# Windowed attention on one core: GpSimd's low part of the exponential waits for VectorE's logits of the same step

## The chip, the cores and the metric

One core of a Trainium2 chip runs the whole program. The metric is the time of one execution in microseconds (us). The engines are TensorE (PE in the profile, its weight loads PEld), VectorE (DVE), ScalarE (ACT), GpSimd (POOL) and SyncE (SP), which here issues DMAs.

## What is computed

The program is a fake-quantised windowed attention on a 16x192x56x56 image, followed by a ConvNeXt block (7x7 convolution, layer norm, two products). The change is in the attention. Cut to that part, the reference is:

```
B, C, H, W = x.shape                      # 16, 192, 56, 56; windows of 7 x 7, 12 heads of 16
q = fq(q * SCALE); k = fq(k); v = fq(v)   # fq: round to 8 bits with one scale for the tensor
attn = jnp.einsum('bhmc,bhnc->bhmn', q, k)
attn = fq(attn) + bias[None]
attn = fq(attn)
attn = jax.nn.softmax(attn, axis=3)
out = jnp.einsum('bhmn,bhnc->bhmc', attn, v)
```

## The kernel before, in words

The program runs seven phases one after another: ranges of the input and of q, k and v, a second pass that writes them quantised, the attention, the output projection, the convolution and the two products of the block. There is no scheduler. Each engine has its own list of instructions, written by hand, and engines meet only at semaphores.

`phase_attention` (L759) works in 512 steps. A tile is two windows at once, on 98 of 128 partitions, with 12 heads x 49 = 588 columns. Each tile goes through a pipeline, and each engine does in step n what is written in its own `step(n, l, stage)`, for tiles of different age:

- PE, in this order: q·k of tile n into `p_psum` (L455), the logits with their maximum taken off of tile n-3 into `l_psum` (L875 to L879), the product with the values of tile n-6 into `o_psum` (L894, 24 matmuls), and the transposes of the logits of tile n-1 into `t_psum` (L903), from which the maximum is taken.
- ACT: the exponential of tile n-4 twice, once in float32 into `exp` (L922, two buffers) and once in float16 into `exp_hi` (L923, four buffers, semaphore `hid`), and then `attn_int` of tile n (L929, semaphore `a1d`), which rounds `p_psum` to 8 bits.
- DVE: `logit_int` of tile n-1 (L948, semaphore `a2d`), which adds the bias to `attn_int`; so the logits of tile n are made at the head of DVE's step n+1. Then the reciprocal of the sums (L957), a statistic of the output (L962), the normalised output `a_o` (L975, semaphore `nrm`) and the negative maximum `neg_max` (L981).
- POOL: `exp_lo = exp - exp_hi` of tile n-4, two instructions (L852, semaphore `lod`), as soon as `exp_hi` of that tile is there. POOL issues nothing else in this phase, no DMA either.

L948 reads two operands from on-chip memory (`attn_int` and `bias_products`), and L852 reads two as well (`exp` and `exp_hi`).

Who waits for `lod`: PE, before it multiplies tile n-6 by the values, and ACT, before it writes `exp` again, since there are only two such buffers. In ACT's step the latter is

```
m, r, bank = n - LAG_E, (l - LAG_E) % 4, (l - LAG_E) % 2
act.wait_ge(lgd, m + 1)
if stage(LAG_E + 2):
    act.wait_ge(lod, m - 1)
```

that is, the `exp` of tile n-4 needs `exp_lo` of tile n-6 (LAG_E is 4). SP loads q, k and v of 16 tiles at a time (a unit) and stores the output of a unit.

Of the kernel before, what the change touches and what calls it, by code (L numbers as in the profile page):

```python
# [60 lines left out]
def chain(eng, sem, start=0):  # L61

    count = [start]

    def link(ins):
        count[0] += 1
        ins.then_inc(sem, 1)
        eng.wait_ge(sem, count[0])
    link.count = count
    return link  # L70
# [47 lines left out]
def col(s, k, rows=P):  # L118
    return s.sc[0:rows, k:k + 1]
# [639 lines left out]
def phase_attention(s):  # L759
# [4 lines left out]
    with ExitStack() as c:  # L764
# [22 lines left out]
        zero, qk, a1d, a2d = s.sem("a_preset"), s.sem("a_qk_done"), s.sem("a1_done"), s.sem("a2_done")  # L787
# [7 lines left out]
        def steps(eng, step):  # L795

            def turn(i, first):
                for k in range(2):
                    for j in range(UP):
                        step(32 * i + 16 * k + j, 16 * k + j, lambda lag: not first or 16 * k + j >= lag)  # L800
            turn(0, True)
            with eng.Fori(0, (IMG - 1) // TURN) as t:
                for m in range(TURN):
                    turn(TURN * t + m + 1, False)
            for j in range(LAG_S):
                step(TAIL + j, j, lambda lag: lag > j)

        @blk.sync
        def _(sp):
            def store(u, k):  # L810
                sp.wait_ge(ostd, u + 1)
                for h in range(2):
                    sp.dma_start(s.od[bass.ds(u, 1)].rearrange("u h n j w f -> (u h) n j w f")[h], o[k][64 * h:64 * h + N]).then_inc(st[k], 16)

            def unit(i, first):
                for k in range(2):
                    u = bass.ds(2 * i + k, 1)
                    if not first:
                        sp.wait_ge(qk, UP * (2 * i + k - 1))
                    load_qk(s, sp, u, q[k], kt[k], ld[k])  # L820
                    if not first:
                        sp.wait_ge(pvd, UP * (2 * i + k - 1))
                    else:
                        sp.wait_ge(vzero, k + 1)
                    for w in range(2):
                        sp.dma_start(vt[k][64 * w:64 * w + N, w], s.vd[bass.ds(2 * i + k, 1)].rearrange("u o n j f -> (u o) n j f")[w]).then_inc(lv[k], 16)
                    if not first:
                        store(2 * i + k - 2, k)
            peeled(sp, IMG, unit)
            for k in range(2):  # L830
                store(UNITS - 2 + k, k)
            for k in range(2):
                sp.wait_ge(st[k], 32 * IMG)

        @blk.gpsimd
        def _(pool):
            link = chain(pool, zero)
            for m in eh:
                link(nc.gpsimd.memset(m[:], 1.0))
                link(nc.gpsimd.memset(m[:, :, 1], 0.0))  # L840
            for m in el:
                link(nc.gpsimd.memset(m[:], 0.0))

            def step(n, l, stage):
                if stage(LAG_E):
                    r, m = (l - LAG_E) % 4, n - LAG_E
                    pool.wait_ge(hid, m + 1)
                    if stage(LAG_E + 4):
                        pool.wait_ge(pvd, m - 3)
                    src = e[r % 2][:].rearrange("p (a b n) -> p b a n", a=2, b=6)  # L850
                    for a in range(2):
                        last = nc.gpsimd.tensor_tensor(el[r][:, :, 2 * a, 0:N], src[:, :, a], eh[r][:, :, 2 * a, 0:N], ALU.subtract)  # L852
                    last.then_inc(lod, 1)
            steps(pool, step)
            pool.wait_ge(ch, 3)
            nc.gpsimd.partition_all_reduce(col(s, T1), col(s, T0), P, RMAX).then_inc(ar, 1)
# [1024 lines left out]
```

## Time and profile before

| | |
|---|---|
| median of 3 runs | 5082.19 us (5073.92 to 5095.0) |
| the profiled execution | 5095.38 us, of which the span from first to last instruction is 5093.7 us |
| the attention's steps | from 1319.3 us to about 2467 us of the span |
| busy over the whole span | PE 79%, DVE 77%, ACT 64%, POOL 30% |
| granted TensorE clock, mean | 0.902 |

The times are of whole executions; the profile is of one of them. An instruction's row gives its start in the span, its duration, its engine and line, and the tiles that it writes and reads. Consecutive instructions of one kind with no idle time between them are merged into one row with their count. "Idle before" in brackets is the time in which the engine stood still just ahead of the row, and behind the arrow stands what ended it. On ACT and DVE an instruction starts a little before the one ahead of it has ended, so that starts lie closer together than durations add up to.

### The profile page before, as it was taken

To read this page: it belongs to the slowest core of one execution; us is meant where nothing else is said; L and a number is where in the kernel's file an instruction comes from. 1 tells how busy PE (TensorE), PEld (TensorE's weight loads), DVE (VectorE), ACT (ScalarE), POOL (GpSimd) and SP (SyncE) were. 2 spreads that over 40 slices of the span, in tenths; PEclk is the share of its full clock that TensorE was granted. 3 is DMA by queue.
4 is the path that set the end of the run, shared out by engine and by line. 5 is a ranking of instruction groups with operands and counts; after the bars stand their busy time and mean duration, and the time that the engine had idled before them with its cause. 6 is when DMAs were issued, how large, how long until landed. Compare 5 with 4: busy or idle time off the path is not lost. (4 is left out here: it accounts for less than half of the span.)

```text
span 5093.7 us, 116728 instructions
## 1 busy us (share of the span) xinstructions
PE 4027.8 (79%) x40394; PEld 2551.1 (50%) x40394; DVE 3922.3 (77%) x7112; ACT 3246.1 (64%) x5602; POOL 1504.5 (30%) x1844
## 2 busy tenths in 40 slices
PE   1687777676688988888456669996689999999999
PEld 1233554454577776777444434443345455554544
DVE  7797999999999999999645520001799999999985
ACT  0675777775698988989355644443556666666663
POOL 0201111111666666666422200001232222222210
PEclk9997777876799999999777779998799999999999
DMA  7773666665333333333277778886122222222212
GB/s 316 203 204 107 160 160 166 159 163 143 79 96 94 91 94 91 94 91 94 74 256 254 279 243 290 278 278 200 63 66 90 87 90 76 76 90 87 90 55 68
DMA packets 227952, 725.18 MB, mean 142 GB/s; under 512 B 30346, under 2 KB 128138, under 8 KB 206794
## 3 DMA queue, kind: packets, MB, share of 16 engines
q1 hardware_dynamic: 203402, 589.58, 39.6%
q0 software_dynamic: 24128, 130.26, 7.1%
q8 instruction: 230, 3.77, 0.3%
q14 instruction: 192, 1.57, 0.1%
HBM read 428.25 MB, written 291.50 MB: 141 GB/s over the span
## 5 line engine op out<-in xcount | busy, mean ns | idle before, releaser
L852 POOL TENSOR_TENSOR exp_lo<-exp,exp_hi 128x294 f16<-128x294 f32 x1024 | 773.1, 782 | 374.8 <-ACT exp_hi L923 374.8
L1613 PE MATMUL out_psum<-gelu_hi,w_parts 128*128 128x448 f16 x2016 | 605.0, 355 | 58.9 <-DVE w_parts L1789 31.5
L1649 ACT ACTIVATE gelu_pair<-h_psum,b_rows,w_unscale 128x448 f32<-128x448 f32 x448 | 324.5, 728 | 412.5 <-PE h_psum L1565 224.7
L1685 DVE BATCH_NORM_STATS2 ln_stats<-z_img 128x6 f32<-128x192 f32 x448 | 126.0, 344 | 566.7 <-DMA z_img<-zd 565.9
L1349 PE MATMUL conv_psum<-c_in,toeplitz 128*128 128x448 f16 (+1 forms) x2304 | 470.4, 366 | 68.9 <-DMA dwb<-in_L_conv_dw_b_dram 68.9
L948 DVE SCALAR_TENSOR_TENSOR logit_int<-attn_int,scalars,bias_products 128x588 f16<-128x588 int8 x512 | 488.2, 954 | 38.6 <-ACT attn_int L929 27.0
L1565 PE MATMUL h_psum<-ln_parts_T,w_hi 128*128 128x448 f16 x2016 | 494.3, 354 | 18.1 <-DVE w_in L1748 16.2
L929 ACT ACTIVATE attn_int<-p_psum,scalars 128x588 int8<-128x588 f32 x512 | 389.4, 761 | 174.7 <-PE p_psum L455 163.7
L1613 PE MATMUL out_psum<-gelu_lo,w_parts 128*128 128x448 f16 x1344 | 475.5, 354 | 0.0
L610 PE MATMUL range_psum<-q_diag,k_diag 128*128 128x196 bf16 x1536 | 275.2, 316 | 227.8 <-DVE p_min L692 225.0
L894 PE MATMUL o_psum<-a_v,exp_hi 128*128 128x34 f16 x6144 | 382.8, 179 | 78.4 <-DVE a_o L975 66.3
L1363 ACT ACTIVATE c_out<-conv_psum,dwb,conv_unscale 128x448 f32<-128x448 f32 x192 | 223.5, 1164 | 315.3 <-PE conv_psum L1349 315.3
L1506 POOL TENSOR_TENSOR ln_parts<-ln_out,ln_parts 128x512 f16<-128x512 f32 x224 | 257.4, 1170 | 504.0 <-DVE ln_parts L1713 504.0
L894 PEld LDWEIGHTS o_psum<-a_v,exp_hi 128*128 128x128 f16 x6144 | 338.0, 96 | 132.9 <-issue 93.3
L922 ACT ACTIVATE exp<-l_psum,scalars 128x588 f32<-128x588 f32 x512 | 388.0, 758 | 24.3 <-PE l_psum L879 13.5
L923 ACT ACTIVATE exp_hi<-l_psum,scalars 128x588 f16<-128x588 f32 x512 | 399.2, 780 | 0.0
L894 PE MATMUL o_psum<-a_v,exp_lo 128*128 128x34 f16 x6144 | 380.4, 178 | 20.4 <-issue 20.0
L1349 PEld LDWEIGHTS conv_psum<-c_in,toeplitz 128*128 128x128 f16 x2304 | 223.8, 98 | 315.3 <-issue 40.0
L650 ACT ACTIVATE qk_i<-qk_psum,qk_quant_scale 128x392 int8<-128x392 f32 x384 | 218.8, 586 | 249.1 <-PE qk_psum L589 241.3
L692 DVE TENSOR_TENSOR p_max<-range_psum,p_max 128x784 f32<-128x784 f32 x384 | 368.2, 959 | 7.2 <-PE range_psum L610 7.2
L692 DVE TENSOR_TENSOR p_min<-range_psum,p_min 128x784 f32<-128x784 f32 x384 | 368.2, 959 | 0.0
L610 PEld LDWEIGHTS range_psum<-q_diag,k_diag 128*128 128x128 bf16 x1536 | 186.7, 155 | 358.2 <-DVE p_min L692 346.4
(313 smaller groups left out, 9901.8 us busy)
## 6 DMA issues: line engine op xcount, KB each, us to landing
k_diag<-kd SPq DMA_DIRECT2D x128, 384.0 KB, 5.0
toeplitz<-gd SPq DMA_DIRECT2D x48, 1024.0 KB, 17.2
yd<-y_out POOLq DMA_DIRECT2D x16, 2880.0 KB, 28.1
c_in<-yd SPq DMA_DIRECT2D x24, 1920.0 KB, 9.4
zd<-c_out POOLq DMA_DIRECT2D x24, 1792.0 KB, 13.8
z_img<-zd SPq DMA_DIRECT2D x16, 2688.0 KB, 9.4
x_chunk<-in_x_dram SPq DMA_DIRECT2D x12, 3136.0 KB, 10.4
x_img<-in_x_dram SPq DMA_DIRECT2D x16, 2352.0 KB, 15.9
```

Of the source, the lines that this page charges most:

```text
L610: last = nc.tensor.matmul(ps[:, x % 2, y // 2, y % 2 * 256:y % 2 * 256 + HG * N], kt[k][:, g].rearrange("p o n -> p (o n)")[:, j::UP], q[k ...
L692: v.tensor_tensor(e[:, g], ps[:, x % 2].rearrange("p a (b c) -> p (a b) c", b=2)[:, :, 0:HG * N], e[:, g], op).then_inc(done, 1)
L852: last = nc.gpsimd.tensor_tensor(el[r][:, :, 2 * a, 0:N], src[:, :, a], eh[r][:, :, 2 * a, 0:N], ALU.subtract)
L894: last = nc.tensor.matmul(po[:, b * PV0:(b + 1) * PV0], x[r][:, b, a:a + 2].rearrange("p a n -> p (a n)"), rhs, start=a == 0 and x is eh, ...
L922: nc.scalar.activation(e[r % 2][:], pl[:, bank, 0:HM], ACT.Exp, scale=col(s, S2))
L923: nc.scalar.activation(eh[r][:, :, 0:3:2].rearrange("p b a n -> p a b n")[:, :, :, 0:N], pl[:, bank, 0:HM].rearrange("p (a b n) -> p a b n ...
L929: nc.scalar.activation(a1[l % 2][:].rearrange("p (g n) -> p g n", g=G), pp[:, 0:G, 0:HG * N], ACT.Copy, scale=col(s, CP)).then_inc(a1d, 1)
L948: v.scalar_tensor_tensor(a2[r][:], a1[(l - LAG_A2) % 2][:], col(s, RAT), s.bpart[:], ALU.mult, ALU.add).then_inc(a2d, 1)
L1349: last = nc.tensor.matmul(out[:, :, lo:hi], tp[k][:, w, ch, 2 - d, :], yi[k][:, :, ch, yy, lo + d:hi + d], start=x == 0 and part == 0, sto ...
L1565: last = nc.tensor.matmul(ph[:, y % 3, 0:TCH], w, xx, start=x == 0, stop=x == 4)
L1613: last = nc.tensor.matmul(po[:, t, 0:TCH], w, hx[:, f, cols], start=f == 0 and x == 0, stop=f == NF - 1 and x == len(steps) - 1)
L1649: nc.scalar.activation(h[y // 2 % 3][:, y % 2], ph[:, y % 3, 0:TCH], ACT.Gelu, scale=k1[:], bias=b1[:, f:f + 1]).then_inc(hd, 1)
```

## The change

In POOL's step, after the wait for `exp_hi` (`hid`) and the wait for a free `exp_lo` buffer (`pvd`), a wait for the logits of tile n (`a2d`, which L948 raises) is added. `stage(0)` holds in all 512 steps but the last eight that drain the pipeline. No instruction of any engine is added, removed or moved otherwise; the two instructions that were L852 become L854.

```
@@ -847,6 +847,8 @@
                     pool.wait_ge(hid, m + 1)
                     if stage(LAG_E + 4):
                         pool.wait_ge(pvd, m - 3)
+                    if stage(0):
+                        pool.wait_ge(a2d, n + 1)
                     src = e[r % 2][:].rearrange("p (a b n) -> p b a n", a=2, b=6)
                     for a in range(2):
                         last = nc.gpsimd.tensor_tensor(el[r][:, :, 2 * a, 0:N], src[:, :, a], eh[r][:, :, 2 * a, 0:N], ALU.subtract)
```

Here m is n-4, so POOL's work on tile n-4 now stands behind VectorE's work on tile n.

## Rows read from the trace of the kernel before

**Rows 1.** Windows view of the attention's steps: busy us (xinstructions) by engine, PEclk, DMA share, GB/s

```profile
1319.30:2467.00 1147.70, 1014.15 (x22498) 827.74 (x22499) 1075.85 (x2618) 1023.79 (x1535) 773.11 (x1024) 0.97 0.35 91
```

**Rows 2.** Groups by line, the attention's steps: xcount | busy us, mean ns | idle before, releasers

```profile
L852 POOL TENSOR_TENSOR exp_lo<-exp,exp_hi 128x294 f16<-128x294 f32 x1024 | 773.1, 782 | 374.8 <-ACT exp_hi L923 374.8
L948 DVE SCALAR_TENSOR_TENSOR logit_int<-attn_int,scalars,bias_products 128x588 f16<-128x588 int8 x512 | 488.2, 954 | 38.6 <-ACT attn_int L929 27.0 <-issue 9.2
...
L957 DVE RECIPROCAL sum_recip<-o_psum 128x12 f32<-128x12 f32 x511 | 113.3, 222 | 30.6 <-PE o_psum L894 29.8
```

**Rows 3.** The line of the logits: duration ns min/median/max, first and last start us

```profile
L948 DVE SCALAR_TENSOR_TENSOR logit_int<-attn_int,scalars,bias_products x512: 814/841/1401, 1319.3 to 2456.6; 128x588 f16<-128x588 int8 x171
```

**Rows 4.** Timeline of DVE, a free step and a held one

```profile
1972.90 0.82 DVE L948 SCALAR_TENSOR_TENSOR logit_int<-attn_int,scalars,bias_products 128x588 f16<-128x588 int8 x1
...
1973.99 0.33 DVE L975 TENSOR_TENSOR a_o<-o_psum,sum_recip 128x192 f32<-128x192 f32 x1
1974.25 0.65 DVE L981 TENSOR_REDUCE neg_max<-t_psum 128x10 f16<-128x490 f16 x1
1974.82 1.06 DVE L948 SCALAR_TENSOR_TENSOR logit_int<-attn_int,scalars,bias_products 128x588 f16<-128x588 int8 x1
...
1976.99 1.06 DVE L948 SCALAR_TENSOR_TENSOR logit_int<-attn_int,scalars,bias_products 128x588 f16<-128x588 int8 x1
```

**Rows 5.** Timeline of POOL at the same place

```profile
1973.84 1.42 POOL L852 TENSOR_TENSOR exp_lo<-exp,exp_hi 128x294 f16<-128x294 f32 x2 [0.77 <-ACT exp_hi L923]
```

**Rows 6.** Timeline of ACT at the same place

```profile
1973.00 0.77 ACT L923 ACTIVATE exp_hi<-l_psum,scalars 128x588 f16<-128x588 f32 x1
1973.89 0.75 ACT L929 ACTIVATE attn_int<-p_psum,scalars 128x588 int8<-128x588 f32 x1
1974.54 0.74 ACT L922 ACTIVATE exp<-l_psum,scalars 128x588 f32<-128x588 f32 x1
1975.18 0.77 ACT L923 ACTIVATE exp_hi<-l_psum,scalars 128x588 f16<-128x588 f32 x1
1975.82 0.75 ACT L929 ACTIVATE attn_int<-p_psum,scalars 128x588 int8<-128x588 f32 x1
```

**Rows 7.** Windows view, an early stretch of 10 us (columns as in rows 1)

```profile
1343.00:1353.00 10.00, 10.00 (x235) 8.22 (x231) 10.00 (x27) 10.00 (x17) 10.00 (x12) 1.00 0.47 100
```

**Rows 8.** Timeline of POOL around that stretch

```profile
1341.73 11.62 POOL L852 TENSOR_TENSOR exp_lo<-exp,exp_hi 128x294 f16<-128x294 f32 x12
```

**Rows 9.** Timeline around one of ACT's waits for POOL

```profile
1366.38 1.42 POOL L852 TENSOR_TENSOR exp_lo<-exp,exp_hi 128x294 f16<-128x294 f32 x2 [0.78 <-ACT exp_hi L923]
1366.43 0.75 ACT L929 ACTIVATE attn_int<-p_psum,scalars 128x588 int8<-128x588 f32 x1
...
1367.82 0.75 ACT L922 ACTIVATE exp<-l_psum,scalars 128x588 f32<-128x588 f32 x1 [0.64 <-POOL exp_lo L852]
```

**Rows 10.** Timeline, POOL released by DVE in a later phase

```profile
4009.78 0.56 DVE L1713 CAST ln_parts<-ln_out 128x768 f16<-128x768 f32 x1
...
4010.42 1.16 POOL L1506 TENSOR_TENSOR ln_parts<-ln_out,ln_parts 128x512 f16<-128x512 f32 x1 [6.71 <-DVE ln_parts L1713]
```

**Rows 11.** Timeline, DVE released by ACT

```profile
1796.27 0.75 ACT L929 ACTIVATE attn_int<-p_psum,scalars 128x588 int8<-128x588 f32 x1 [4.08 <-PE p_psum L455]
...
1797.06 0.83 DVE L948 SCALAR_TENSOR_TENSOR logit_int<-attn_int,scalars,bias_products 128x588 f16<-128x588 int8 x1 [0.35 <-ACT attn_int L929]
```

**Rows 12.** Timeline, from DVE's normalised output over PE to ACT's next rounding

```profile
2200.10 0.34 DVE L975 TENSOR_TENSOR a_o<-o_psum,sum_recip 128x192 f32<-128x192 f32 x1
...
2200.59 0.18 PE L894 MATMUL o_psum<-a_v,exp_hi 128*128 128x34 f16 x1 [0.23 <-DVE a_o L975]
...
2201.47 0.43 PE L455 MATMUL p_psum<-q_diag,k_diag 128*128 128x196 bf16 x3
...
2201.93 0.75 ACT L929 ACTIVATE attn_int<-p_psum,scalars 128x588 int8<-128x588 f32 x1
```

**Rows 13.** Waits over the attention's steps: us in total, times, longest us

```profile
POOL exp_lo L852 <- ACT exp_hi L923: 374.8, 423, 9.0
...
ACT exp L922 <- POOL exp_lo L852: 1.0, 2, 0.6
```

More of the change, by code:

```diff
@@ L849, in step @@
                         pool.wait_ge(pvd, m - 3)
+                    if stage(0):
+                        pool.wait_ge(a2d, n + 1)
                     src = e[r % 2][:].rearrange("p (a b n) -> p b a n", a=2, b=6)
```

## The prediction

> **What bounds the kernel now.** I read the windows view first, to see how full each engine is in the attention [rows 1]. The change touches nothing outside these 1148 us of the span. VectorE (DVE) is busy in 1076 of them, ScalarE (ACT) in 1024, TensorE (PE) in 1014, GpSimd (POOL) in 773. So DVE sets the pace, ACT stands close behind it, and POOL has room.
>
> The timeline gives the pace. A step of DVE with nothing in its way goes from one L948 to the next in 1974.82 - 1972.90 = 1.92 us [rows 4]; I use 1.93. ACT's own three instructions give the same: from L923 at 1973.00 over L922 at 1974.54 to L923 at 1975.18 the starts are 0.64 to 0.65 us apart when nothing intervenes, 3 x 0.64 = 1.92 [rows 6]. But the first L948 starts at 1319.3 and the last at 2456.6 [rows 3], 1137.3 us for 511 intervals, 2.226 each. The line groups say where the other 0.30 us goes [rows 2]:
>
> - L948 takes 488.2 us in 512 instructions. At 0.825 each, which is the free one of [rows 4] (0.82 to 0.83), that would be 422.4. **Excess: 66 us.**
> - DVE stands idle before L948 for 38.6 us and before L957 for 30.6, together 69. These are few and long stalls, in which PE or everything stands; the change does not address them.
> - 511 x 1.93 + 66 + 69 = 1121. The last 16 us are the extra instructions at the end of each unit and roundings.
>
> The step without stalls is (1137.3 - 69) / 511 = 2.09 us.
>
> The excess comes from POOL. POOL began a pair of L852 at 1973.84 and ended it at 1975.26 [rows 5]. DVE's L948 began at 1974.82 and ended at 1975.88, 1.06 instead of 0.825 [rows 4]. It behaves as if it had begun at 1975.88 - 0.825 = 1975.05, which is 0.21 us before the end of POOL's pair. L948 waits for POOL, and the overlap that is allowed is 0.21 us. The other order exists too: from 1343 to 1353 POOL and DVE both show busy for all of 10.00 us [rows 7], and POOL's 12 instructions there take 11.62 us, 0.97 each [rows 8] instead of 1.42 / 2 = 0.71. There POOL is the one held, and a pair lasts a step of 1.94, the free pace of DVE.
>
> The Trainium skill (SBUF — State Buffer, Who interferes with whom) says that a VectorE instruction with two SBUF inputs and a GpSimd instruction that reads SBUF exclude one another, and that whichever was issued first makes the other wait. By that rule, these traces agree in kind; its "for the whole instruction" is weighed below.
>
> **The change part by part.** It removes and moves no instruction. It adds one wait per step on POOL. L852 of tile n-4 now begins after DVE's L948 of tile n.
>
> *What it removes.* POOL no longer is under way when the L948 begins that follows its `exp_hi`; the order in which POOL blocks DVE by beginning just before it is gone. If that were all, 66 us would come back. What remains is the next L948. After a free one there are 1.93 - 0.83 = 1.10 us to it. POOL's pair begins 0.08 us after (a POOL instruction released by DVE: DVE's CAST ended at 4010.34, POOL began 4010.42 [rows 10]), lasts 1.42 [rows 5] and lets L948 go 0.21 before its end: 0.08 + 1.42 - 0.21 = 1.29 us. That is later than 1.10. So the port alone gives a step of 0.83 + 1.29 = 2.12 us, against 2.09 now: the contention moves from one side of the pair to the other, and nothing is won.
>
> *What it adds.* The wait is never free. POOL begins now when `exp_hi` is there (423 of its idle times end so [rows 13]), 0.07 us after L923: 1973.77 to 1973.84 [rows 5, 6]. In the same step ACT begins L929 of tile n only at 1973.89 and ends it at 1974.64, and L948 of it follows. Undisturbed, that L948 could end at 1974.82 + 0.83 = 1975.65, and POOL would begin at 1975.73 instead of 1973.84, 1.9 us later. Behind POOL's waiting instruction stand only its next pairs, no DMA. Two engines wait for `lod`:
>
> - PE's product of tile n-4 with the values is two steps later, and it also stands behind the normalised output L975 of the tile before it. POOL's pair ends 1.50 us after L948 of tile n, while that L975 comes a step and some 0.6 us after it. It does not wait.
> - ACT's L922 writes `exp` of tile n-2 two steps later, into the buffer that POOL reads. It does wait, and this is the new chain. Now that chain is slack: it ended ACT's idle time twice, 1.0 us in all [rows 13], and the one in [rows 9] shows what it is like: POOL's pair ends at 1367.80, L922 begins at 1367.82.
>
> The new chain closes on itself over two steps: L922 to L929, L929 to L948, L948 to POOL, POOL to the L922 of two steps later. From the rows:
>
> - L922 begins at 1974.54, L929 at 1975.82: 1.28 [rows 6]
> - L929 itself: 0.75 [rows 6]
> - its end to L948: 1797.02 to 1797.06, 0.04 [rows 11]
> - L948, free: 0.83 [rows 4]
> - its end to POOL: 0.08 [rows 10]
> - the pair: 1.42 [rows 5]
> - its end to L922: 0.02 [rows 9]
>
> Sum 4.42 us for two steps, **2.21 us a step**. That is above 2.12 (port), 1.93 (DVE and ACT), so it is the pace. Does anything slip into the chain? L929 needs PE's q·k of its tile, which comes behind L975: from the end of L975 at 2200.44 to L929 at 2201.93 it takes 1.49 us [rows 12]. L975 ends some 0.6 us after L948 (1973.72 to 1974.32 [rows 4]). So q·k of tile n+2 is there 0.6 + 1.49 = 2.1 us after the end of L948 of tile n, and L929 of tile n+2 begins 0.08 + 1.42 + 0.02 + 1.28 = 2.80 after it. 0.7 us of cover are left; without it each 0.1 us would cost 0.05 us a step, 26 us in all.
>
> **The sum.** Steps: 511 x 2.21 = 1129. Stalls: all 69 us stay in full at the upper end. PE and DVE now have slack of 0.3 to 0.7 us in a step, so each stall loses up to that. The waits of [rows 2] fall in few steps; I take 30 stalls of half a microsecond, an estimate, 15 us, which leaves 54. 1129 + 54 = 1183, and with a few us at the 32 unit ends, now covered, left at 4, 1187. Against 1137: **+50 us**. On the profiled execution that is 5095.4 + 50 = 5145 us. That execution lies at the upper end of the three runs; on their median it is 5082 + 50 = 5132, which I predict.
>
> Bounds: the latency from POOL to ACT was seen once at 0.02; the other releases in the rows are 0.04 to 0.08 us, so the chain is 4.40 to 4.50, 2.20 to 2.25 a step. Low: 511 x 2.20 + 40 = 1164, +27. High: 511 x 2.25 + 69 = 1219, +82. That is 5109 to 5164.
>
> **The rivals.**
>
> - *The wait costs what it saves, no change.* If ACT's buffer chain had more slack than I read, the port's 2.12 us would be the pace: 511 x 2.12 + 54 = 1137, that is 5082, up to 5097 with all stalls kept. For it: the pace of now is also set by that port. Against: the `lod` wait of ACT counts tiles and can't be passed, and [rows 9] shows it binding, for 0.64 us; here POOL is 1.9 us later than before. It decides only if the chain is under 4.24 us, 0.18 below my sum. 0.12.
> - *Faster.* The mechanism is the one of [rows 7, 8], POOL held or behind but DVE at the free pace: 1.93 to 2.00 us a step and the stalls as now give back up to the 66 us of excess, 5016 to 5052. For it: the excess is real and its cause is the overlap. Against: it needs POOL's pair out of the way within 1.10 us of L948's end, and it needs 1.29; and ACT must not wait. The point from which it decides is a pair of 1.2 us or a third `exp` buffer, which the change does not bring. 0.06.
> - *Clearly slower than forecast.* L948 is held until POOL's pair has ended, with no 0.21 us of overlap: 0.83 + 0.08 + 1.42 = 2.33 us a step, 511 x 2.33 + 69 = 1260, +123, 5205. [rows 4, 5] speak against it: the overlap is measured. PE falling into the chain (0.7 us of cover, above) would look the same in the time. 0.10. The Trainium skill (same page and section) has the pair of ports held for the whole instruction, which is this case; the trace has the held L948 end 0.21 us too early for it.
> - *Forecast*, POOL late and ACT waiting for it, 2.20 to 2.25 us a step: 0.72, 5109 to 5164.
>
> That the wait does nothing is excluded: L929 of tile n comes after L923 of tile n-4 on the same engine, so L948 of tile n always ends after POOL could begin.
>
> **How the numbers follow.** The runs before spread over 0.4%, so what can be told from no change is about 0.5%, 25 us: below 5057 is faster, above 5108 slower. Forecast and the slow rival are slower but for the low edge of the forecast (0.02); the first rival gives 0.12 to no change. Faster 0.06, same 0.14, slower 0.80. The range takes in the upper edge of no change (5097) and leaves out the faster and the far slower case: 5098 to 5168.
>
> **What the profile would show.** Right: POOL's L854 released by DVE `logit_int` in nearly all its idle times, no longer by `exp_hi`; L948 (now L950) near 0.83 us on average, its busy time down from 488 to about 425 to 435 us; ACT's L922 (now L924) idle for `exp_lo` in most steps, 2.21 - 1.93 = 0.28 us each, some 140 us in all; starts of L950 2.21 us apart; the same stalls. Wrong: ACT idle for PE's `p_psum` in most steps (PE in the chain), L950 still at 0.95 or more (the port sets the pace), or a step of 1.93 to 2.05 us. What would make the prediction wrong above all is a slip in which tile the wait is for, since one step less would leave 2 us of cover.

## The result and the profile after

| | before | after |
|---|---|---|
| median of 3 runs, us | 5082.19 | 5152.26 (5138.59 to 5162.68) |
| ratio after / before | | 1.0125, 95% interval 1.0106 to 1.0143 |
| the profiled execution's span, us | 5093.7 | 5136.4 |
| first to last start of `logit_int`, us | 1137.3 | 1200.6 |

The change makes the kernel 1.25% slower, which is 64 us of the median of before, with an interval of 54 to 73 us; the two medians of three runs differ by 70 us. In the trace the difference is all in the attention: 1200.6 - 1137.3 = 63.3 us. The span of the profiled execution grew by only 43 us, since its phases behind the attention took some 20 us less than in the profile of before; the change does not reach them, and the three times of a kernel differ by 20 us and more among themselves.

The groups by line in the attention's steps answer to [rows 2] (columns: xcount | busy us, mean ns | idle before, releasers):

```profile
L854 POOL TENSOR_TENSOR exp_lo<-exp,exp_hi 128x294 f16<-128x294 f32 x1024 | 723.6, 730 | 488.0 <-DVE logit_int L950 478.2 <-ACT exp_hi L925 3.4 <-issue 3.2
L950 DVE SCALAR_TENSOR_TENSOR logit_int<-attn_int,scalars,bias_products 128x588 f16<-128x588 int8 x512 | 435.6, 851 | 126.4 <-ACT attn_int L931 95.4 <-issue 14.6
L924 ACT ACTIVATE exp<-l_psum,scalars 128x588 f32<-128x588 f32 x512 | 384.6, 751 | 128.2 <-issue 90.6 <-POOL exp_lo L854 10.3 <-PE l_psum L881 8.1
L931 ACT ACTIVATE attn_int<-p_psum,scalars 128x588 int8<-128x588 f32 x511 | 381.6, 747 | 36.9 <-PE p_psum L455 36.6
```

POOL is released by the logits and no longer by `exp_hi`. L950 is back at 0.85 us on average, from 0.954: 53 of the 66 us of excess are gone. In their place VectorE (DVE) stands idle for 126 us before L950, and ScalarE (ACT) for 128 us before L924. The profile puts most of ACT's wait down to "issue". The timeline shows what it is; it answers to [rows 4 to 6]:

```profile
1659.21 0.75 ACT L924 ACTIVATE exp<-l_psum,scalars 128x588 f32<-128x588 f32 x1 [0.33 <-PE l_psum L881]
...
1660.50 0.74 ACT L931 ACTIVATE attn_int<-p_psum,scalars 128x588 int8<-128x588 f32 x1
...
1661.28 0.83 DVE L950 SCALAR_TENSOR_TENSOR logit_int<-attn_int,scalars,bias_products 128x588 f16<-128x588 int8 x1 [0.34 <-ACT attn_int L931]
...
1662.19 1.42 POOL L854 TENSOR_TENSOR exp_lo<-exp,exp_hi 128x294 f16<-128x294 f32 x2 [0.94 <-DVE logit_int L950]
...
1663.40 0.83 DVE L950 SCALAR_TENSOR_TENSOR logit_int<-attn_int,scalars,bias_products 128x588 f16<-128x588 int8 x1
...
1663.69 0.75 ACT L924 ACTIVATE exp<-l_psum,scalars 128x588 f32<-128x588 f32 x1 [0.33 <-issue]
```

Read it as a chain. L924 begins at 1659.21, L931 at 1660.50, ends at 1661.24; L950 begins at 1661.28 and ends at 1662.11; POOL's pair begins at 1662.19 and ends at 1663.61; L924 of two steps later begins at 1663.69, 0.08 after it. 4.48 us for two steps, 2.24 each. The starts of L950 are mostly 2.36 and 2.12 us apart in turn; in 318 of 510 cases two steps together take 4.46 to 4.50 us. Counted by tiles, L924 begins 0.08 to 0.11 us after the end of the pair it waits for, that of two tiles before, in 470 of 510 tiles, among them 238 of the 245 whose wait is labelled "issue". Those are waits for POOL. In the kernel before, L922 never begins less than 0.24 us after that pair. The shorter interval is what the port allows: the L950 at 1663.40 begins 0.21 us before the end of POOL's pair. (It also begins 0.03 us after the end of the L931 at 1662.62, so ScalarE lets it go at the same moment.)

### The profile page after: what moved, and what is told of

The parts are those of the page before. It is cut to its first block and busy times, and to the rows that moved or that the text cites. A ratio compares the mean times of both kernels' runs of the same rounds, so it can differ in the third digit from the quotient of the medians.

```text
span 5136.4 us, 116791 instructions
## 1 busy us (share of the span) xinstructions
PE 4026.8 (78%) x40394; PEld 2546.3 (50%) x40394; DVE 3905.2 (76%) x7112; ACT 3264.8 (64%) x5602; POOL 1454.2 (28%) x1844
## 5 line engine op out<-in xcount | busy, mean ns | idle before, releaser
L854 POOL TENSOR_TENSOR exp_lo<-exp,exp_hi 128x294 f16<-128x294 f32 x1024 | 723.6, 730 | 488.0 <-DVE logit_int L950 478.2
L950 DVE SCALAR_TENSOR_TENSOR logit_int<-attn_int,scalars,bias_products 128x588 f16<-128x588 int8 x512 | 435.6, 851 | 126.4 <-ACT attn_int L931 95.4
L924 ACT ACTIVATE exp<-l_psum,scalars 128x588 f32<-128x588 f32 x512 | 384.6, 751 | 128.2 <-issue 90.6
L931 ACT ACTIVATE attn_int<-p_psum,scalars 128x588 int8<-128x588 f32 x512 | 382.3, 747 | 113.3 <-PE p_psum L455 113.1
L925 ACT ACTIVATE exp_hi<-l_psum,scalars 128x588 f16<-128x588 f32 x512 | 387.8, 757 | 0.0
L1567 PE MATMUL h_psum<-ln_parts_T,w_lo 128*128 128x448 f16 x1344 | 366.0, 354 | 0.0
```

Of the source, the lines that this page charges most:

```text
L924: nc.scalar.activation(e[r % 2][:], pl[:, bank, 0:HM], ACT.Exp, scale=col(s, S2))
L925: nc.scalar.activation(eh[r][:, :, 0:3:2].rearrange("p b a n -> p a b n")[:, :, :, 0:N], pl[:, bank, 0:HM].rearrange("p (a b n) -> p a b n ...
L931: nc.scalar.activation(a1[l % 2][:].rearrange("p (g n) -> p g n", g=G), pp[:, 0:G, 0:HG * N], ACT.Copy, scale=col(s, CP)).then_inc(a1d, 1)
L950: v.scalar_tensor_tensor(a2[r][:], a1[(l - LAG_A2) % 2][:], col(s, RAT), s.bpart[:], ALU.mult, ALU.add).then_inc(a2d, 1)
L1567: last = nc.tensor.matmul(ph[:, y % 3, 0:TCH], w, xx, start=x == 0, stop=x == 4)
```

## The experiments

"Steps" is the time from the first to the last start of `logit_int` (L948 before), "usual step" the commonest distance of those starts, or distances where there are several. Ratios are against the kernel before, on the same chip, with their 95% interval; two kernels were run once.

| run | ratio | steps, us | usual step, us | `logit_int`, mean us |
|---|---|---|---|---|
| before | 1 | 1137.3 | 1.93 to 2.4, mixed | 0.954 |
| after | 1.0125 (1.0106 to 1.0143) | 1200.6 | 2.11 and 2.36 | 0.851 |
| after_four_exp | 1.0040 (1.0019 to 1.0060) | 1160.6 | 2.11 | 0.969 |
| before_four_exp | 0.9994 (0.9977 to 1.0012) | 1137.6 | mixed | 0.943 |
| wait_between | 1.0040 (1.0020 to 1.0059) | 1157.3 | 2.12 | 0.973 |
| wait_one_earlier | 1.0025 (1.0005 to 1.0046) | 1152.1 | 2.12, with 1.93 and more mixed in | 0.977 |
| start_four_exp | 0.9904 (0.9877 to 0.9931) | 1093.8 | 1.93 | 0.849 |
| start_two_exp | 1.0082 (1.0062 to 1.0102) | 1191.1 | 1.93, 2.32, 2.52 | 0.979 |
| start_between | 0.9919 (0.9898 to 0.9939) | 1099.0 | 1.93 | 0.851 |
| start_between_four | 0.9919 (0.9891 to 0.9948) | 1093.9 | 1.93 | 0.848 |
| after_half_pair | one run, 5042.5 us | 1101.3 | 1.93 | 0.825 |
| before_half_pair | one run, 5020.0 us | 1091.7 | 1.93 | 0.823 |

**Is it the chain through the two `exp` buffers?** The changed kernel with four of them:

```
-        e = [sb(f"exp{k}", [P, HM], F32) for k in range(2)]
+        e = [sb(f"exp{k}", [P, HM], F32) for k in range(4)]
...
-                    if stage(LAG_E + 2):
-                        act.wait_ge(lod, m - 1)
+                    if stage(LAG_E + 4):
+                        act.wait_ge(lod, m - 3)
```

with `e[r]` for `e[r % 2]` where ACT writes and POOL reads.

> The changed kernel with four exp buffers in place of two, so that ScalarE's L924 no longer waits for GpSimd's pair of two steps before, but of four. Theory (chain): the pace of the changed kernel, 2.24 us a step (2.11 and 2.36 in turn), is set by the two-step chain L924, L931, L950, pair, L924. With the chain cut the port is next: 0.83 + 0.08 + 1.42 - 0.21 = 2.12 us a step, 511 x (2.24 - 2.12) = 61 us less than the changed kernel, ratio to the kernel before 0.997 to 1.004; starts of L950 an even 2.11 to 2.13 apart. Rival (port alone sets the pace already) or rival (TensorE in the chain): no difference to the changed kernel, ratio 1.012.

It is. 0.85% come back, 40 us in the steps, and the usual step is the port's 2.11 us; the ratio stands at the upper edge of what was expected. DVE's timeline there:

```profile
1869.61 1.00 DVE L950 SCALAR_TENSOR_TENSOR logit_int<-attn_int,scalars,bias_products 128x588 f16<-128x588 int8 x1
1871.72 1.01 DVE L950 SCALAR_TENSOR_TENSOR logit_int<-attn_int,scalars,bias_products 128x588 f16<-128x588 int8 x1
```

L950 is held again, 1.00 us in place of 0.83: with ACT out of the way DVE is ready before POOL's pair ends. The saving was expected at 61 us, and 40 came. What lies above the usual step, stalls and the ends of units, is 1160.6 - 511 x 2.115 = 80 us here and 1200.6 - 511 x 2.24 = 56 us in the changed kernel. Most of that difference lies in the intervals of over 3 us, the long stalls: 25 of them hold 56 us above the usual step here, 17 hold 39 us in the changed kernel. That the idle time of DVE there hid a part of the stalls is my reading of it; no run isolates it.

The same edit to the kernel before:

> The kernel before with four exp buffers in place of two, nothing else. Theory: the buffers' chain is slack there (it ended two of ScalarE's idle times), so ratio 0.998 to 1.002 and L948 still at 0.95 us on average. Rival (the two buffers held the kernel before back as well, so that the gain of the other run is no sign of the change's chain): ratio 0.99 or lower.

No difference (0.9994). The buffers held nothing back before the change. So the chain is made by the change.

**Does it matter where POOL waits for the end of the logits?** Once between the two instructions of the pair, once for the logits of the tile before. Both kernels have two `exp` buffers. The first cut is against the kernel before, so no wait stands ahead of the pair; the second is against the changed kernel:

```
                     for a in range(2):
+                        if a == 1 and stage(0):
+                            pool.wait_ge(a2d, n + 1)
```

> The wait for the logits of tile n stands between the two instructions of GpSimd's pair instead of ahead of both. Theory: the first one runs while ScalarE rounds and ends 0.1 us ahead of the point at which it would hold L950; the second begins 0.08 us after L950. The chain over two steps is 0.80 + 0.08 + 1.28 + 0.75 + 0.04 + 0.83 = 3.78 us, 1.89 a step, so VectorE's and ScalarE's own 1.93 set the pace: L950 at 0.83 us, the 66 us of excess given back, ratio 0.985 to 0.990. Rival (the port needs L950 and the whole pair in turn, 2.12 us a step, wherever the wait stands): ratio 1.00 to 1.003. Rival (a wait on GpSimd costs by itself): slower than before.

```
                     if stage(0):
-                        pool.wait_ge(a2d, n + 1)
+                        pool.wait_ge(a2d, n)
```

> The wait is for the logits of tile n-1 instead of tile n. These end about as ScalarE's exp_hi of the same step does (1973.72 against 1973.77 in the trace of before), so the wait seldom holds anything. Theory (which tile is waited for is the whole cost): ratio 0.995 to 1.003, GpSimd released by exp_hi in most steps. Rival (the wait itself, or any tie of GpSimd to VectorE, costs): 1.01 as in the changed kernel.

The first was a miss, and the instructive one. I expected 1.93 us a step, it is 2.12, the rival's number. The timeline of wait_between:

```profile
1860.53 1.41 POOL L854 TENSOR_TENSOR exp_lo<-exp,exp_hi 128x294 f16<-128x294 f32 x2 [0.70 <-DVE logit_int L950]
...
1861.56 1.00 DVE L950 SCALAR_TENSOR_TENSOR logit_int<-attn_int,scalars,bias_products 128x588 f16<-128x588 int8 x1
...
1862.64 1.42 POOL L854 TENSOR_TENSOR exp_lo<-exp,exp_hi 128x294 f16<-128x294 f32 x2 [0.70 <-DVE logit_int L950]
...
1863.67 1.01 DVE L950 SCALAR_TENSOR_TENSOR logit_int<-attn_int,scalars,bias_products 128x588 f16<-128x588 int8 x1
```

POOL waits for the end of L950, does the second half, and the first half of the next tile is then already due and follows without a gap. Two instructions stand between two L950 again, only not those of one tile. My sum had the first half run in ACT's shadow; it left out that POOL, once late, is always late. (L924 begins 0.08 us behind POOL here too, in 434 of 510 tiles, but that chain has slack: L931 ends at 1861.25, L950 begins only at 1861.56.) The second run, expected at 0.995 to 1.003, is at 1.0025, inside; but my reason for it, that POOL would be released by `exp_hi`, was wrong. The waits of wait_one_earlier:

```profile
POOL exp_lo L854 <- DVE logit_int L950: 239.3, 321, 3.3
...
POOL exp_lo L854 <- ACT exp_hi L925: 142.1, 81, 9.0
```

Its commonest step is 2.12 too, 212 of 511, but 101 are under 1.98 us. In the kernels in which POOL waits for the end of L950 and the chain does not set the pace, the commonest step is this one: L950, 0.08 us of hand-over, 1.42 of POOL, less 0.21. Steadily so in after_four_exp and wait_between, 311 and 346 of 511 steps.

**Then the hand-over is the dear part.** In [rows 7, 8] steps are 1.93 us long although POOL is held in every one. There it is the port that hands over, not a semaphore. Can POOL be made to arrive just behind L950? It waits for what lets L950 start, in place of its end: `neg_max` of DVE's step ahead of it (`mxd`) and `attn_int` of tile n (`a1d`). The cut is against the changed kernel; the four `exp` buffers of above are in this kernel as well:

```
                     if stage(0):
-                        pool.wait_ge(a2d, n + 1)
+                        pool.wait_ge(mxd, n - 1)
+                        pool.wait_ge(a1d, n + 1)
```

> GpSimd's pair waits, in place of the end of L950 (logits of tile n), for the two things that let L950 start: neg_max of VectorE's step ahead of it (mxd at n-1) and attn_int of tile n (a1d at n+1); four exp buffers. Theory (the hand-over by semaphore is the dear part): L950 starts at once behind both, GpSimd some 0.1 us after it and is held by the port until 0.16 us before the end of L950 (in the trace of before a pair's second half issued at 1966.56 under an L948 of 1966.46 to 1967.29 ended at 1967.87, so it began 0.16 before that end), in place of beginning 0.08 us after it. Port loop 0.83 - 0.16 + 1.42 - 0.21 = 1.88 us, under VectorE's own 1.93: L950 at 0.83 us, steps of 1.93, ratio 0.985 to 0.990. Rival (port loop of 2.12 us however GpSimd is released): ratio 1.00 to 1.004 and steps of 2.11.

Faster than the kernel before: 0.9904. The steps are 1.93 us, L951 (the logits here) 0.849, and POOL's instructions are the ones that are held, 0.915 us on average where they take 0.73 in the changed kernel. The groups by line and the timeline of start_four_exp:

```profile
L855 POOL TENSOR_TENSOR exp_lo<-exp,exp_hi 128x294 f16<-128x294 f32 x1024 | 914.2, 915 | 189.8 <-ACT attn_int L932 93.2 <-issue 52.9 <-DVE neg_max L984 31.6
L951 DVE SCALAR_TENSOR_TENSOR logit_int<-attn_int,scalars,bias_products 128x588 f16<-128x588 int8 x512 | 434.5, 849 | 41.6 <-ACT attn_int L932 28.4 <-issue 9.6 <-PE l_psum L882 0.4
```

```profile
1728.68 0.82 DVE L951 SCALAR_TENSOR_TENSOR logit_int<-attn_int,scalars,bias_products 128x588 f16<-128x588 int8 x1
1728.98 1.12 POOL L855 TENSOR_TENSOR exp_lo<-exp,exp_hi 128x294 f16<-128x294 f32 x1
```

POOL's first instruction begins 0.30 us behind L951 and ends at 1730.10. Of itself it takes 0.74, so it had the port from 1729.36, and L951 ended at 1729.50: POOL goes on 0.14 us *before* the end of L951, where the semaphore gives 0.08 us *after* it. 471 of POOL's instructions are held in this way behind an L951 of 0.83 us, with a median of 0.14 us. The port's own hand-over comes earlier than the semaphore's by 0.14 + 0.08 = 0.22 us a step: 2.12 - 0.22 = 1.90, under DVE's own 1.93. The attention gets 1137.3 - 1093.8 = 43.5 us shorter, not the 66 us of excess that I expected back.

The Trainium skill (SBUF — State Buffer, Who interferes with whom) says that the order of issue decides which of the two is blocked. By that rule, the trace agrees at a lead of 0.30 us. The cheap order is the one in which GpSimd is blocked, 1.93 against 2.12 us a step, since it has the room. The Trainium skill's "for the whole instruction" (same section) is 0.14 to 0.21 us too long at either change of hands here.

With the two buffers of before:

> As start_four_exp, with the two exp buffers of the kernel before. Theory: the two-step chain through the buffers is (1.28 + 0.75 + 0.04 + 0.83 - 0.16 + 1.42 + 0.08) / 2 = 2.12 us a step, so ratio 1.00 to 1.004 against the kernel before, ScalarE's L924 waiting for exp_lo; 0.012 to 0.015 above start_four_exp. Rival (the buffers are no matter here): the same as start_four_exp.

The buffers matter, 1.0082 against 0.9904 with four. But the size is a miss: 2.25 us a step on average among those without stalls and not 2.12. The steps come mostly in threes, 1.93, 2.32 and 2.52, and in 141 of 512 steps L951 takes 1.3 to 1.4 us. The timeline of start_two_exp at such a step:

```profile
1765.25 0.75 ACT L932 ACTIVATE attn_int<-p_psum,scalars 128x588 int8<-128x588 f32 x1
1766.03 1.41 DVE L951 SCALAR_TENSOR_TENSOR logit_int<-attn_int,scalars,bias_products 128x588 f16<-128x588 int8 x1 [0.31 <-ACT attn_int L932]
1766.07 1.94 POOL L855 TENSOR_TENSOR exp_lo<-exp,exp_hi 128x294 f16<-128x294 f32 x2 [0.27 <-PE o_psum L897]
```

Both are released by the end of L932 at 1766.00. For POOL I read that from the time, 0.08 us later, as POOL begins behind ACT and DVE elsewhere; the profile's label names a product of PE. DVE begins 0.04 us ahead of POOL, and still POOL has the port first, so at this distance the recorded starts do not tell which is blocked. With four buffers ACT is seldom late, L951 mostly follows `neg_max` with no gap, and the POOL instruction that is held comes mostly 0.16 to 0.33 us behind. Over the four kernels with this kind of wait I counted the steps in which POOL's instruction begins within 0.75 us after L951 (this distance is DVE's lead) and no other is under way: in all 177 with a lead of 0.035 to 0.045 us L951 was held, in all 383 with a lead of 0.051 us or more it was not. Only five of the 383 have a lead under 0.09 us, so the limit is thinly sampled there. How much of the 2.25 us the held L951 make up was not isolated.

The start waits between the two halves, with two and with four buffers:

> The two waits of start_two_exp stand between the first and the second instruction of the pair, two exp buffers. Theory: the second instruction is held by the port until 0.16 us before the end of L950, ends 0.58 after it, the next first one begins behind it or 0.08 us after its exp_hi. Port loop 1.88 to 1.91 us, chain (1.28 + 0.75 + 0.04 + 0.83 + 0.58 + 0.08) / 2 = 1.78: steps of 1.93, ratio 0.985 to 0.990. Rival (port loop 2.12 us): 1.00 to 1.004, as wait_between.

> start_between (the waits for neg_max and attn_int stand between the two instructions of the pair) with four exp buffers as well. Theory: steps are already VectorE's own 1.93 us in start_between and in start_four_exp, so the two cures don't add: ratio 0.988 to 0.993, L951 near 0.85. Rival (stalls are recovered faster with more buffers and an earlier first half): 0.985 or lower.

0.9919 both, 1.93 us a step both, within the intervals of start_four_exp. So there are two ways to the same pace, more buffers or a pair divided around L951, and they don't add. start_between was expected at up to 0.990, the times are a little above.

**Is the excess of L948 POOL's hold at all?** The second instruction of POOL's pair is left out, in both kernels (the low part of the exponential of the second window is missing):

```
-                    for a in range(2):
+                    for a in range(1):
```

> The kernel before without the second instruction of GpSimd's pair (the low part is left out for the second window). Theory (the excess of L948 in the kernel before is GpSimd's hold on the port): the pair becomes 0.74 us, begins at exp_hi and is over before L948 of the same step starts, so L948 at 0.83 us (excess under 10 of 66 us) and steps of 1.93, a span some 50 to 65 us under 5094. Rival (L948 is slow for another reason, its own operands or ScalarE): the excess stays near 66 us.

> The changed kernel without the second instruction of GpSimd's pair (the low part is left out for the second window; its buffer stays zero there). Theory (chain): the two-step chain loses 0.69 us, 4.48 - 0.69 = 3.79, 1.9 a step, the port loop too (0.83 + 0.08 + 0.73 - 0.21 = 1.43), so VectorE's own 1.93 us sets the pace, L950 at 0.83, the span about 511 x (2.24 - 1.94) = 150 us under the changed kernel's 5136. Rival (TensorE's wait for the normalised output or for L950 sets the pace of the changed kernel): steps stay at 2.2 or more.

The line of the logits, first in before_half_pair, then in after_half_pair (duration ns min/median/max, first and last start us), to be read beside [rows 3]:

```profile
L948 DVE SCALAR_TENSOR_TENSOR logit_int<-attn_int,scalars,bias_products x512: 814/822/862, 1318.4 to 2410.1; 128x588 f16<-128x588 int8 x171
```

```profile
L950 DVE SCALAR_TENSOR_TENSOR logit_int<-attn_int,scalars,bias_products x512: 819/825/833, 1319.4 to 2420.7; 128x588 f16<-128x588 int8 x171
```

Not one of 512 instructions is held, and the longest takes 0.86 us where it was 1.40. So the excess is POOL's hold, and all of it goes. But the time does not give back all of it: the steps of the kernel before get 46 us shorter, not 66, and those of the changed kernel 99, to 1.93 a step. (The span of the one run of before_half_pair is 75 us under 5094, where 50 to 65 were expected; 46 of them are in the steps.) I expected 150 for the second. My sum took what lies above the usual step to stay the same, and it did not: 1101.3 - 511 x 1.93 = 115 us, where the changed kernel has 56. TensorE's order is the same in all these kernels, so it is not what holds the changed one at 2.24.

## Why the prediction was right

The forecast was 5132 us in a range of 5098 to 5168; measured 5152. Against the +50 of the forecast stand +70 between the medians and +63 in the steps of the trace. The parts below are held against the trace; the rest, 7 us, is within the interval of the result. By its steps:

- *The excess and its cause*: 66 us in L948, from POOL's hold. before_half_pair shows it: it all goes. "If that were all, 66 us would come back" was too much: 46 us of time came back there, and 43.5 in start_four_exp.
- *The port keeps what it gives*: 2.12 us a step, "the contention moves from one side of the pair to the other, and nothing is won". after_four_exp shows 2.11 to 2.12 once the chain is cut. What the prediction did not say is that this holds for a wait on the *end* of L948 alone; the 0.08 us behind it is 0.22 us later than the port's own hand-over. I had that in [rows 7, 8] and took it for a rival that needs a shorter pair or a third buffer. It needed a wait on something earlier, and as for the buffer that was right for the pair taken whole.
- *The chain*: five of its seven terms are within 0.01 us (L931 0.74 to 0.75, its hand-over 0.04, L950 0.83, POOL's 0.08, the pair 1.42), and L924 to L931 is 1.29 for 1.28. The mis-sized term is the last, "its end to L922: 0.02": it is 0.08 (1663.61 to 1663.69). The one row that I had for it [rows 9] is not such a hand-over, and I misread it. The L922 at 1367.82 is the 23rd, of tile 22, and waits for the pair of tile 20. That pair is the first line below; it ended at 1365.60, 2.2 us before. The pair that ends at 1367.80 is that of tile 21. What came last is PE's product of tile 22, at 1367.33 + 0.45 = 1367.78, 0.04 us ahead of L922:

```profile
1364.19 1.41 POOL L852 TENSOR_TENSOR exp_lo<-exp,exp_hi 128x294 f16<-128x294 f32 x2 [0.49 <-ACT exp_hi L923]
...
1367.33 0.45 PE L879 MATMUL l_psum<-ident_f,neg_max 128*64 128x128 f16 x10 [0.69 <-issue]
```

  So [rows 9] does not show ACT's wait for POOL binding "for 0.64 us", as the argument against the rival "no change" has it, and the profile's two waits of [rows 13] are of this kind: with 0.24 us as the least distance, no L922 of the kernel before waited for POOL. That the new chain would bind rested on the wait in the program and on the 1.9 us alone, and that held. With the right term, 4.48 / 2 = 2.24 in place of 2.21, 0.03 x 511 = 15 us: 50 + 15 = 65, against 63 in the trace.
- *Stalls and unit ends*: forecast 54 + 4 = 58 us, in the trace 56 by the same reckoning. Its two parts were not measured apart, and the 30 stalls of half a microsecond were a guess, so that the sum comes out so near is in part luck.
- *TensorE's cover*: L931 idles 36.9 us, nearly all for `p_psum` and in 28 waits; it stays out of the chain, as forecast.
- *What the profile would show*: L950 busy 435.6 us, forecast 425 to 435; L924 idle 128.2 us, of which 112 ahead of the 470 that follow POOL's pair, forecast some 140; POOL released by `logit_int` 501 times. The profile labels ACT's waits "issue" more often than POOL, which I had not foreseen.

Among the rivals, "no change" would have needed a chain under 4.24 us and it is 4.48; L950 held for the whole of the pair would show in 2.33 us a step where the port sets the pace, and after_four_exp has 2.11 there.

## What to carry to other kernels

When two engines share a port, count both ways of handing it over: a semaphore on the end of the instruction came 0.22 us later here than the port itself, and that in nearly every step. A wait that orders two engines is best put on what lets the favoured one start, with a lead that is safe (nothing from 0.051 us up lost here, and nearly all of those were 0.09 or more), so that the engine with room is the one held. And before an engine off the critical path is delayed, follow each buffer that it frees around its ring: with two `exp` buffers 1.9 us of delay closed a loop of 4.48 us, with four it closed none. Last, a releaser that the profile names is an inference from times: count the tiles before a wait is priced by it. Here the two waits of the kernel before that were labelled as POOL's were not POOL's, and 238 of the changed kernel that were labelled "issue" were.

## What the runs showed of the hardware

- Two instructions that exclude each other still overlap by some tenths: L948 goes on 0.20 to 0.21 us before POOL's ends (225 held ones in the kernel before, 404 L950 in after_four_exp), POOL's goes on 0.14 to 0.16 us before L951's or L948's ends.
- A lead of up to 0.045 us at the recorded start does not win the port for DVE (177 of 177 steps), one of 0.051 us or more does (383 of 383). A wait for one and the same event on both engines gave just the losing lead: DVE begins 0.03 us behind the end of L932, POOL 0.08.
- The kernel before never settles in one order: it drifts between the step of 1.93 us, POOL held, and those of 2.1 to 2.4, L948 held. With a wait of POOL for the end of L950 the commonest step is 2.12 or above, with one for its start it is 1.93 but for start_two_exp; wait_one_earlier still has 101 steps of 511 under 1.98.
